# Two rings of PSUM banks in attention: turned sums and minus-maximum move into them, and maxima are interleaved with scores by duration

## The reference

```
layer 0: scores = q k^T / 4, allowed where 0 <= i - j < 64   (window of 64)
layer 1: scores = q k^T / 4, allowed where j <= i            (causal, q and k rotated)
out = softmax(scores) v          batch 4, sequence 1024, heads 16
```

## Time and profile before

| | us |
|---|---|
| three runs | 2669.9, 2677.19, 2673.15 |
| their median | 2673.15 |
| the profiled execution, its own time | 2665.74 |
| its span | 2663.9 |
| mean granted TensorE clock (share of 2.4 GHz) | 0.816 |

### The profile page before, as it was taken

One profiled execution on the slowest core, in us unless ns is written; L12 is line 12 of the kernel. 1 busy time (PEld: TensorE's weight loads), 2 busy tenths in 40 slices (PEclk: granted clock), 3 DMA queues, 4 the chain that ended last, 5 costly groups with the idle time before them and its releaser, 6 DMA issues. The chain is left out here.

```text
span 2663.9 us, 50684 instructions
## 1 busy us (share of the span) xinstructions
PE 1990.6 (75%) x15004; PEld 1261.7 (47%) x15005; DVE 1566.4 (59%) x3203; ACT 1125.7 (42%) x2280; POOL 779.5 (29%) x954
## 2 busy tenths in 40 slices
PE   5997899755889999970596999999998240299950
PEld 2772334544779999960352223323225130177740
DVE  3654556574555666645595777767755774155556
ACT  2652556453544444420351566656664442033310
POOL 1453677125700000017363112221110235400026
PEclk8996899855689999995796788988888555599985
DMA  4234443024621111124235122212100115222244
GB/s 136 108 131 129 135 129 97 15 80 173 209 69 48 47 47 47 50 81 132 95 134 155 36 65 64 65 54 62 48 1 15 44 49 184 104 83 83 83 154 146
DMA packets 194992, 239.08 MB, mean 90 GB/s; under 512 B 25700, under 2 KB 154500, under 8 KB 194340
## 3 DMA queue, kind: packets, MB, share of 16 engines
q1 hardware_dynamic: 176836, 183.16, 21.9%
q0 software_dynamic: 17696, 54.02, 6.0%
q10 hardware_dynamic: 320, 0.16, 0.0%
HBM read 132.90 MB, written 103.84 MB: 89 GB/s over the span
## 5 line engine op out<-in xcount | busy, mean ns | idle before, releaser
L820 DVE TENSOR_REDUCE a_mx<-a_pmx 128x1 f32<-128x512 f32 (+2 forms) x960 | 507.7, 575 | 262.3 <-PE a_pmx L720 212.5
L907 ACT ACTIVATE a_probs<-a_pst 128x512 f32<-128x512 f32 (+3 forms) x928 | 433.2, 522 | 299.9 <-PE a_pst L735 297.7
L1926 POOL DMA_INDIRECT m_got<-m_ys_d,m_slot x128 | 128.3, 1002 | 770.0 <-issue 769.4
L1789 PE MATMUL m_ph<-m_zh,m_w 128*128 128x256 f16 x2808 | 322.9, 274 | 18.1 <-DVE m_zh L1867 17.9
L1803 PE MATMUL m_py<-m_w,m_zh 128*128 x2808 | 319.4, 273 | 0.5 <-DVE x_res L1863 0.3
L1789 PEld LDWEIGHTS m_ph<-m_zh,m_w 128*128 x2808 | 272.7, 98 | 59.9 <-issue 25.6
L710 PE MATMUL a_pmx<-a_Ks,a_Qs 48*128 48x192 f16 (+4 forms) x1280 | 258.4, 330 | 48.9 <-DMA a_V<-v_d 33.0
L1803 PEld LDWEIGHTS m_py<-m_w,m_zh 128*128 128x128 f16 x2808 | 268.5, 98 | 35.8 <-issue 2.3
L854 POOL TENSOR_SCALAR_AFFINE_SELECT a_probs<-a_probs 128x512 f32<-128x512 f32 x256 | 162.7, 636 | 396.4 <-ACT a_probs L907 395.1
L747 PE MATMUL a_pacc<-a_probs,a_V 128*32 128x128 f32 (+5 forms) x2688 | 258.8, 459 | 10.2 <-ACT a_oT L897 3.6
L735 PE MATMUL a_pst<-a_Qs,a_Ks 50*128 50x192 f16 (+5 forms) x1344 | 251.0, 309 | 19.7 <-DMA a_Qs<-a_nmp 10.7
(11 more groups left out here) (208 smaller groups left out, 2952.1 us busy)
## 6 DMA issues: line engine op xcount, KB each, us to landing
xs_d<-a_zero POOLq DMA_DIRECT2D x26, 768.0 KB, 4.5
m_zh<-xs_d SPq DMA_DIRECT2D x78, 256.0 KB, 2.7
m_ys_d<-x_res SPq DMA_DIRECT2D x78, 256.0 KB, 2.2
v_d<-p_vt SPq DMA_DIRECT2D x16, 1024.0 KB, 4.5
parts_d<-p_part SPq DMA_DIRECT2D x64, 256.0 KB, 2.6
a_V<-v_d SPq DMA_DIRECT2D x32, 512.0 KB, 3.9
a_Qs<-parts_d SPq DMA_DIRECT2D x192, 64.0 KB, 2.3
a_Ks<-parts_d SPq DMA_DIRECT2D x192, 64.0 KB, 2.2
```

What stands on the lines that cost most here:

```text
L820: nc.vector.tensor_reduce(mx[:, par % 2, part, hs[0]:hs[0] + len(hs), i], src, AX.X, ALU.max, negate=True).then_inc(m_done, 1)
L907: nc.scalar.activation(probs[:, (hg * NV + v) % NPB, h:h + per, q0:q1], src, ACT.Exp, scale=HD ** -0.5 / QK_SCALE ** 2).then_inc(exp_done, 1)
L1789: mm = nc.tensor.matmul(ph[:, (G * par + g) % 4, q * ROWS:(q + 1) * ROWS], self.w1[:, bass.ds(e, 1), c, wp, m * P:(m + 1) * P].rearrange(" ...
L1926: pool.indirect_dma_start(got[:, t % NG, k, :], None, self.ys_d[:, :], bass.IndirectOffsetOnAxis(ap=self.slot[:, k, t:t + 1], axis=0)).the ...
```

## The change

- `pst` keeps three banks, `pmx` gets four; `pms` is gone. nmT takes a place in the ring of `pst`, the two transposes of sums (oT) one each in the ring of `pmx`. The bank of a unit is its place in the ring, counted over the steps, modulo 3 or 4. `free_s` and `free_m` work out which unit had the bank and wait for exp, for `act_nm`, for the reduction or for `dve_norm`.
- S units are issued in twos: `pe_st` does units u and u + 1, which belong to the two halves of rows.
- M and E pairs are placed where their summed cost, reckoned as columns plus 64 for each unit, keeps step with the summed cost of exp. Of 22 pairs, `EARLY` = 10 are now E in layer 1 (12 M), and 5 of 8 in layer 0 (3 M).
- nmT comes where 0.08 (layer 1) or 0.16 (layer 0) of all exp cost has gone by since the last M.

The diff, cut to its core:

```diff
-            NB = 3
-            pst = self.ps(ctx, T + "pst", [P, NB, 512])
-            pmx = self.ps(ctx, T + "pmx", [P, NB, 512])
+            NBS, NBM = 3, 4
+            pst = self.ps(ctx, T + "pst", [P, NBS, 512])
+            pmx = self.ps(ctx, T + "pmx", [P, NBM, 512])
             pacc = self.ps(ctx, T + "pacc", [P, 512])
-            pms = self.ps(ctx, T + "pms", [P, 512])
...
+            for v in range(NV):
+                seq += [("st", u) for u in of_v[v][::2]]
+                seq.append(("pv", v - LATE))
...
+            EARLY = round(NP * (0.45 if layer else 0.6))
+            TURN = 0.08 if layer else 0.16
+            order = list(range(EARLY, NP)) + list(range(EARLY))
+            dve_cost = [2 * (heads_of(2 * p) * (maxu[2 * p][3] - maxu[2 * p][2]) + 64) for p in order]
+            act_cost = lambda u: 2 * (expu[u][6] * (expu[u][4] - expu[u][3]) + 64)
...
+                act_sum += act_cost(item[1])
+                while m < NP and (dve_sum + dve_cost[m] / 2) * act_all <= act_sum * dve_all:
+                    plan.append(("max", order[m]) if m < NP - EARLY else ("early", order[m]))
...
+                if nm_at is not None and act_sum > nm_at + TURN * act_all:
+                    plan.append(("nmT", 0))
...
+            def free_s(pe, par, s, unit):
+                ago, r = before(par, ring_s.index(unit), RS, NBS)
...
+                if kind == "st":
+                    pe.wait_ge(exp_done, NE * (s - ago) + u + 1)
+                else:
+                    pe.wait_ge(nmp_ready, s - ago + 2)
+
+            def free_m(pe, par, s, unit):
+                r = ring_m.index(unit) - NBM
...
+                elif kind == "oT":
+                    pe.wait_ge(norm_done, 2 * (s - ago) + 2 - a)
+                else:
+                    n = NM + 2 * EARLY + NM * (s - ago) + nth_max[r] + 1
...
+                    pe.wait_ge(m_done, n)
...
-            LAG = 4
-            plan, m, due = [], 0, None
-            for n, item in enumerate(seq):
-                plan.append(item)
-                while m < NP and m * len(seq) < (n + 1) * NP:
-                    plan.append(("max", EARLY + m) if m < NP - EARLY else ("early", m - NP + EARLY))
...
-                        pe.wait_ge(norm_done, 2 * s + 1 - a)
-                        if a == 0 and nmT_first and ahead > 0:
-                            pe.wait_ge(nmp_ready, s + 2)
-                        pe_oT(pe, s - a, a)
+                        free_m(pe, par, s, (kind, a))
+                        pe_oT(pe, s - a, a, bank_m(par, (kind, a)))
```

More of the change, by code:

```diff
@@ L661, in attend @@
             twice_v = [v for v in range(NV) if len(cuts[v][1]) == 2]
[L663 to L670, removed]
+            LATE = 2
+            seq = []
+            for v in range(NV):
+                seq += [("st", u) for u in of_v[v][::2]]
+                seq.append(("pv", v - LATE))
+                if v == LATE:
+                    seq.append(("oT", 1))
+                if v == E0 + LATE:
+                    seq.append(("oT", 0))
@@ new lines, in attend, with bank_s, bank_m, before @@
+            RS, RM = len(ring_s), len(ring_m)
+            assert SETS * RM % NBM == 0
+            nth_max = [sum(kind != "oT" for kind, _ in ring_m[:r]) for r in range(RM)]
+            def bank_s(par, unit):
+                return (par * RS + ring_s.index(unit)) % NBS
+            def bank_m(par, unit):
+                return (par * RM + ring_m.index(unit)) % NBM
+            def before(par, at, length, banks):
+                ring = [(q * length + r) % banks for q in range(SETS) for r in range(length)]
+                g = par * length + at
+                n = next(n for n in range(1, 2 * banks) if ring[g - n] == ring[g])
+                return (0, at - n) if n <= at else (1, at - n + length)
@@ L714, in pe_max @@
                 if diag:
[L715 to L719, removed]
+                    nh = len(hs)
+                    wide = P if layer else cols
+                    m = mask[:, 0, :] if layer else mask[:, 0, 2 * P - cols:2 * P]
@@ L726, in pe_nmT, with pe_st @@
                 mm.then_inc(nmT_done, 1)
[L728 to L737, removed]
+            def pe_st(pe, par, s, first):
+                for u in (first, first + 1):
+                    c, k, j, q0, q1, h0, per = expu[u]
+                    free_s(pe, par, s, ("st", u))
+                    g0, g1 = c * HALF + q0, c * HALF + q1
+                    for n in range(per):
+                        mm = nc.tensor.matmul(pst[:, bank_s(par, ("st", u)), n * (q1 - q0):(n + 1) * (q1 - q0)], rows(Ks, par, h0 + n, KAUG)[:, j * P:(j + 1) * P],
+                                              rows(Qs, par, h0 + n, KAUG)[:, g0:g1], start=True, stop=True, skip_group_check=True)
+                    mm.then_inc(st_done, 1)
@@ L860, in pool_step @@
                 for kind, a in plan:
-                    v = next((v for v in cut_v if kind == "st" and a == of_v[v][-1]), None)
+                    v = next((v for v in cut_v if kind == "st" and a + 1 == of_v[v][-1]), None)
                     if v is not None:
```

148 lines of the change are left out of this document (86 added, 62 removed).

## The result

The changed kernel ran in 2573.03 us (median of four runs, 2570.72 to 2575.22) against 2673.59 for the kernel before on the same chip: ratio 0.963, 95% interval 0.9608 to 0.9652. The forecast was 2597, with a range of 2560 to 2648. The profiled execution took 2571.12 us, its span is 2569.3, 94.6 less than before's.

The account below looks back on a forecast made before the run. Layer 1 was held by three in-order queues waiting for each other and a falling clock, layer 0 by SP's loop; 63 + 3 + 4 + 5 + 1 = 76 us off gave 2597 on the median, range 2560 to 2648.

Parts of the forecast that it names:

- Layer 1's steps: Fourteen layer-1 steps: each goes from 34.0 to 29.5 us, 63 us in all.
- nmT later: Layer 1: more PE work ahead of nmT removes its wait for POOL, 0.6 us a step.
- the clock: Layer 1: filling the weak stretch before nmT and shrinking bank gaps recovers 1.9 of 2.3 us a step.
- The fourth bank: Layer 1: a whole pair can be written while the one before is reduced, cutting DVE's idle time, 2.0 us a step.
- S in twos: Layer 1: saved slots, 1.6 us of PE in all, inside the bank's 2.0; a possible loss counted out against it.
- Rings shared: Layer 1: turned sums and minus-maximum in the rings cost 0, bounds 0 and 1.5 us a step.
- Before layer 1's first step: The 33 pairs ahead of layer 1's steps become 32 and DVE may run through: 4 us, bounds 1.3 and 8.
- Layer 0: 3 us before its first step and 5 in its steps, bounds -11 and 20; SP's loop holds at 14.1.
- The dips: First rival: layer 1's low clock before nmT stays, as long gaps alone would cause drops; 2624 on the median, chance 0.23.
- S12 to pv3: Second rival: layer 1's clock falls earlier in this stretch, at DVE's pace, and costs more; 2688 on the median, chance 0.07.
- its floor: Rival: four banks hide all handoffs, DVE is idle 2 us a layer-1 step of 27.0; 2562 on the median, chance 0.13.
- the banks: Rival: the banks weren't it, PE waits as often for ACT's three; everything within 0.3%, about 2670, chance 0.07.

Follow-up runs that it names:

- X3: The kernel before with one number changed: in layer 1 nmT stands six items after nm, not four; 2628.3 us, ratio 0.985.
- X1: The order of the kernel before put into the changed kernel's rings, four banks for M, E and turned sums; 2628.7 us, ratio 0.9851.
- X4: X1 with nmT six items after nm, not four, in both layers, S still single; 2587.6 us, ratio 0.969.
- X5: The changed kernel with M and E placed by count, S in twos kept, nmT after S22.23; 2577.6 us, ratio 0.9656.
- X7: The changed kernel with layer 1's nmT moved ahead, right after the first pair S and E0 behind nm; 2627.7 us, ratio 0.9846.
- X2: X1 with every M, E and turned sum waiting for the reduction three places back, as with three banks; 2680.1 us, ratio 1.0033.
- X6: The changed kernel with each M, E and turned sum waiting for the reduction three places back, not four; 2669.6 us, ratio 0.9991.
- X12: X11 with layer 0's load of V issued behind the four sends of minus-maximum, not ahead of them; 2565.84 us, ratio 0.9611.
- X9: The changed kernel with each pv of a four-pair unit cut into two halves of two heads; ratio 0.972, 25 us slower than the change.
- X11: The changed kernel with layer 1 ordered as in X4 and layer 0 left as in the change; 2570.53 us, ratio 0.9636.

## Why the prediction was right, and where it wasn't

**The total.** The sum was 76 us off the profiled execution, and 94.6 came off. The medians gave 2573.03 for 2597: inside the range of 2560 to 2648, but below the 2578 to 2615 that the forecast gave its own case. Layer 1's fourteen steps came out as forecast; the miss is in the rest, 13 us forecast and 32 measured: the stretch before step 1 (8 us more than its term), layer 0 (3 more), what lies behind layer 1's last nmT (3.6 for 1), and 5 us outside attention that no run explains.

**Layer 1's steps.** 63 us forecast, 62.6 measured, at the forecast clock (over 0.97) and with the holds of M's weight loads for DVE under 30 us. That it fits within 0.4 us is luck: the bank, and nmT with the clock, were worth 10 us more than their terms, and the order in twos and by duration lost 10 that the sum had at nothing. And the terms were divided wrongly.

- *nmT later, 0.6, and the clock, 1.9.* I priced them as two. They are largely one: X3 moved nmT alone and brought 2.7 us a step, of which 0.6 is the wait, and the rest came with the clock; with four banks (X1 to X4) it brought 3.2. The term "nmT later" should have carried the clock with it.
- *The fourth bank, 2.0.* In the old order 2.3 a step, some of it clock (0.90 to 0.92): well sized. With nmT late already it brought 2.5 (X3 to X4), in the change's order 5.6. Its size depends on the order around it, which a single number can't say.
- *S in twos, a gain inside the 2.0.* Wrong sign in layer 1: 0.5 a step lost. The loss that I had "counted out" (the second S waits for exp and holds M behind it) is larger than the slots saved (the waits of PE for exp in X5 and X4).
- *Placing by duration.* Worth nothing in layer 1 (0.2 a step lost). What matters of the change's order there is that nmT stands late: behind S22.23 and E0 alone it brings the low clock back (X7), and behind S23 but ahead of pv4 it does as well as in the change (X4).
- *Rings shared, 0.* Some 0.2 a step (X2), though the turned sums do wait for DVE in the change.

By these runs the 62.6 are: nmT's place 37.9, bank and rings behind it 34.9, twos -7.5, by duration -2.7.

**Before layer 1's first step.** 4 forecast, bound 8, measured 12.4: mis-sized, and outside its bounds. X2 against X1 gives 14, X6 against the change 10.4, so it is the bank. I had counted the bank's handoffs only while pairs are large. But the clock is at 1.2 GHz there, PE's part of each handoff takes twice as long, and DVE went from 74% to 89% busy (48.64 of 65.80, 47.31 of 53.40). The clock also came back sooner: before, it was at 0.50 for all of the 65.8 us, after for the first 42.7 of the 53.4, in X6 for the first 52.8 of 63.8.

**Layer 0.** 3 and 5 forecast, 10.9 measured. Stall gone, more waiting for the sends, SP's loop as the bound: all seen, and X12 shows the loop to be the bound. Not so that PE's order hardly enters it: with SP's queue left as it was the steps took 250.3 us in X1, 245.9 in X5 and 239.6 in the change, and the loop of 14 us went to 13.45 in the step shown. The loop runs through PE, from the sends' landing to the last pv.

**The rivals.** The dips did not stay: 0.88 became 0.99. This goes against the Trainium skill's rule of long gaps, cited with the first rival. No clock fell in S12 to pv3, DVE did not reach its floor (24.4 of 29.6 us), and the banks did matter. One drop is left in the fourteen steps of the change, at the loop's back-edge (timeline: start, length, idle before; then a window):

```profile
1690.94 0.51 PE L824 MATMUL a_pst<-a_Qs,a_Ks 50*128 50x512 f16 x2 [2.95 <-issue]
```
```profile
1692.00:1694.00 2.00, 1.53 (x10) 0.62 (x13) 1.36 (x4) 1.92 (x4) 0.01 (x1) 0.50 0.16 51
```

PE stands 2.95 us for nothing that the profile shows, the clock is at 0.50 behind it, and this step is 7 us longer than its neighbours, in the kernel before too (its gap there is 2.1 us). A longer gap does the same, then, but in these kernels it is the rare case.

## What to carry to other kernels

Waits of 0.3 to 2 us at one fixed place of a step can cost two to four and a half times their length, with PE's clock that falls there (24.1 us of waits cost 48.7 in X7, 8.5 cost 37.9 in X3): price a stall together with the clock in the windows behind it, and try the one-number move of that instruction before rebuilding the order. Test an edit of several parts in both directions, since a bank was worth 2.3 us a step in one order and 5.6 in the other, and two of the parts were worth nothing or less in layer 1, where most of the gain was, and paid in layer 0. Where small urgent DMAs share a queue with a large one that is not urgent, put the large one behind them, but only as much as its own reader can wait for.

## What the runs showed of the hardware

- pv of two heads takes 1.05 us and of four heads 1.07 (X9): cutting a group that runs together saves nothing.
- A 4 KB send landed in 1.8 us without a 512 KB load issued just ahead of it and in 2.7 with it (X12, X11).
- Two orders with the same waits of M for three banks (X3: 12.7 and 78.6 us; X6: 17.1 and 65.5) ran at clocks of 0.96 and 0.90. In X6 S waits for exp besides (17.7 us, in X3 0.6), and the falls begin where two pairs M stand in a row; how much each does stays open.
